# Layer 0's scaling of x reads the second copy of x, and the first copy's load waits for the dot products alone

## The reference, cut to what matters

```python
x = x_input                                   # (32, 512, 128)
e = (x @ a_i)[:, :, None] + (x @ a_j)[:, None, :]
mean = e.mean(axis=(1, 2)); var = ((e - mean) ** 2).mean(axis=(1, 2))
e = (e - mean) * rsqrt(var + 1e-14) * adj + adj
e = where(e >= 0, e, 0.2 * e)
alpha = softmax(e, axis=1)
h = sigmoid(einsum('bij,bjd->bid', alpha, x))
x = layernorm(x + h)
# layer 1: masked attention, a second aggregation and a small MLP, + x, layernorm
# layer 2: two projections mixed by a matrix made of adj, + x, layernorm
# layer 3: masked attention, elu, + x, layernorm
```

## Time and profile before

| what | value |
|---|---|
| median of the runs | 1194.18 us (1192.84 to 1195.81, 3 runs) |
| span of the profiled execution | 1188.6 us, 28920 instructions |
| TensorE matmul busy | 1103.5 us (93%) |
| VectorE busy | 1055.8 us (89%) |
| ScalarE busy | 964.7 us (81%) |
| GpSimd busy | 594.6 us (50%) |
| mean granted TensorE clock | 0.972 of full speed |
| loads of xA and xrA | 32 each, 256 KB, median 2.9 and 2.7 us to landing |

### The profile page before, as it was taken

How to read it: one execution, slowest core, us unless ns; L and a number is a source line. 1 busy time by engine, 2 the same in 40 slices (tenths; PEclk the granted TensorE clock), 3 DMA queues, 4 the chain that set the end, 5 groups by cost and what they waited for, 6 DMA issues and landing times.

```text
span 1188.6 us, 28920 instructions
## 1 busy us (share of the span) xinstructions
PE 1103.5 (93%) x7752; PEld 907.9 (76%) x7752; DVE 1055.8 (89%) x3894; ACT 964.7 (81%) x2453; POOL 594.6 (50%) x1250
## 2 busy tenths in 40 slices
PE   4779999999999999999999999999999999999964
PEld 3457777888777888887778888877778888788743
DVE  6887999999999999999999999999999899997642
ACT  3566888888888888888888889888888898888753
POOL 4243435555564555556555555555545554553422
PEclk7799999999999999999999999999999999999976
DMA  3010001110011111000111110101111010010000
GB/s 76 19 36 19 27 28 46 31 31 22 22 35 35 35 35 35 26 28 17 35 35 35 35 35 26 35 9 35 35 35 35 29 37 30 17 46 10 28 9 19
DMA packets 59478, 36.17 MB, mean 30 GB/s; under 512 B 3872, under 2 KB 54816, under 8 KB 59424
## 3 DMA queue, kind: packets, MB, share of 16 engines
q1 hardware_dynamic: 59424, 35.54, 10.0%
HBM read 18.75 MB, written 8.39 MB: 23 GB/s over the span
## 4 chain that ended last, share of the span: by engine, by line
PE 58%; POOL 10%; issue 9%; DVE 5%; ACT 2%; DMA 1%; POOLq 0%; SPq 0%; ACTq 0%; DVEq 0%
PE ps L965 14%; PE ps L893 7%; PE ps L949 6%; PE ps L982 4%; PE ps L1025 4%; PE ps L934 4%; PE ps L744 4%; PE ps L737 3%; POOL rirA L559 2%; PE ps L1014 2%; PE ps L880 2%; PE ps L1043 2%; PE ps L1042 2%; PE ps L919 1%; DMA xA<-in_x_dram 1%
## 5 line engine op out<-in xcount | busy, mean ns | idle before, releaser
L965 PE MATMUL ps<-hE,pTE 128*128 128x128 f32 x1024 | 131.0, 277 | 0.2
L982 PE MATMUL ps<-gin_j,hgat 128*128 128x512 f32 x256 | 124.4, 610 | 3.0 <-DVE gin_j L1495 1.8
L965 PE MATMUL ps<-hB,pTB 128*128 128x128 f32 x1024 | 125.3, 275 | 0.7 <-DVE pTB L1626 0.6
L893 PE MATMUL ps<-xsA,pA 128*128 128x128 f32 x1024 | 124.4, 275 | 0.0
L965 PEld LDWEIGHTS ps<-hE,pTE 128*128 128x128 f32 x1024 | 122.8, 193 | 0.9 <-issue 0.6
L1025 PE MATMUL ps<-att_j,xD 128*128 128x512 f32 x256 | 122.3, 601 | 0.8 <-ACT xD L2207 0.8
L965 PEld LDWEIGHTS ps<-hB,pTB 128*128 128x128 f32 x1024 | 119.4, 192 | 1.4 <-DVE pTB L1626 1.1
L893 PEld LDWEIGHTS ps<-xsA,pA 128*128 128x128 f32 x1024 | 119.4, 192 | 0.4 <-issue 0.3
L2250 ACT ACTIVATE pA<-vA,nmA,rirA 128x512 f32<-128x512 f32 x128 | 107.0, 845 | 6.3 <-DVE vA L1683 5.3
L2312 ACT ACTIVATE pE<-wE,mnE 128x512 f32<-128x512 f32 x128 | 92.4, 723 | 20.9 <-DVE mnE L1613 20.8
L1595 DVE SCALAR_TENSOR_TENSOR wE<-ps,hE,y2E 128x512 f32<-128x512 f32 x128 | 92.1, 739 | 13.8 <-ACT y2E L2282 13.7
(11 more groups left out here) (238 smaller groups left out, 3084.6 us busy)
## 6 DMA issues: line engine op xcount, KB each, us to landing
xA<-in_x_dram SPq DMA_DIRECT2D x32, 256.0 KB, 2.9
xrA<-in_x_dram SPq DMA_DIRECT2D x32, 256.0 KB, 2.7
xrB<-xB SPq DMA_DIRECT2D x32, 256.0 KB, 2.3
out_dram<-xout SPq DMA_DIRECT2D x32, 256.0 KB, 2.3
adj_i<-in_adj_dram SPq DMA_DIRECT2D x1, 1024.0 KB, 5.5
a<-in_L_gnn_a_dram SPq DMA_DIRECT2D x2, 64.0 KB, 5.1
w_sb<-in_L_gnn_W_dram SPq DMA_DIRECT2D x2, 64.0 KB, 3.7
l2w<-in_L_gnn_W_dram SPq DMA_DIRECT2D x2, 64.0 KB, 3.2
```

The lines of the kernel that those rows point to most:

```text
L893: last = mm(at("aggA")[:, i * P:(i + 1) * P], pA[:, j, i * P:(i + 1) * P], xsA[:, j], start=(j == 0), stop=(j == NT - 1))
L965: last = mm(at("agg" + n)[:, i * P:(i + 1) * P], att[n]["pT"][:, i, j], att[n]["h"][:, j, 0:P], start=(j == 0), stop=(j == NT - 1))
L982: last = mm(at("gin"), hgat[:, j], gin_j[:, j], start=(j == 0), stop=(j == NT - 1))
```

## The change

`load_xA` loses its wait for the scaling of the graph before. `scale_xA` reads xrA instead of xA, and waits for the load of xrA of its own graph. All orders of all engines stay as they are. Both copies hold the same data.

```diff
             def load_xA(g):
                 sp.wait_ge(s["stA_ready"], g.last)
-                sp.wait_ge(s["xA_scaled"], g.last)
                 sp.dma_start(xA[:], x_v[g.g]).then_inc(s["xA_in"], 16)
...
             def scale_xA(g):
                 act.wait_ge(s["rzA"], g.now)
+                act.wait_ge(s["xrA_in"], 16 * g.now)
                 act.wait_ge(s["aggA_ready"], g.last)
                 for j in range(NT):
-                    last = a.activation(xsA[:, j], xA[:, j], ACT.Copy, scale=rzA[:, j:j + 1])
+                    last = a.activation(xsA[:, j], xrA[:, j], ACT.Copy, scale=rzA[:, j:j + 1])
                 last.then_inc(s["xA_scaled"], 1)
```

## The result

The changed kernel takes 1197.66 us (median of 12 runs, 1193.45 to 1199.36), the kernel before 1193.18 us in the runs beside it (12 runs, 1189.72 to 1195.81). The ratio is 1.0039 with a 95% interval of 1.0026 to 1.0051, or 4.7 us slower (4.5 us by the two medians). In a second set of runs it was 1.0044 (1.0028 to 1.0059). The change makes the kernel slower by somewhat more than the 0.3% that can be told from none.

The account below looks back on a forecast made before the run. Prediction: TensorE, busy 93% of the span, bounds the kernel, so only its waits matter. Terms -0.3 - 0.9 + 1.9 + 3.2 - 0.2 give +3.7 us, +5.4 with one clock fall: 1199.6 us, range 1195.0 to 1203.1.

Parts of the forecast that it names:

- The rest around the span: Whole run: the median 1194.18 us exceeds the profiled span of 1188.6 us by 5.6 us, left unchanged in the forecast.
- The two stalls: Scalings of graphs 5 and 29 wait for late xrA, idle about 3 and 4 us: net +1.9 and +3.2 us.
- The terms for this piece: Behind the loop: graph 29's stall +3.2 us, a share of the +1.7 us clock fall, earlier xA for graphs 28 and 29 -0.2.
- Before the loop: Entry to the loop: graph 5's earlier xA -0.9 us, its scaling's stall +1.9 us, a share of the +1.7 us clock fall.
- Graph 5's earlier load: Before the loop: xA no longer waits for graph 4's scaling; gain between 0.57 and 1.25 us, taken as -0.9 us.
- The clock: TensorE's two new pauses: a fall to half clock costs 1.7 us; 0 to 3.4 us for both, one fall taken.
- The loop: Steady loop: xA's load leaves about 0.4 us sooner, but TensorE hardly waits for it; 0 to -1.2 us, taken as -0.3.
- a wait before L1656: Sign in the loop: VectorE would wait before the sum of squares instead, as its xA wait falls from 13.2 to under 5 us.

Follow-up runs that it names:

- e4: Changed kernel plus 14 extra matmuls on TensorE before its wait for graph 29's scaling, two waits exchanged: 1197.64 us, ratio 1.0017 to the kernel before.
- e3: Changed kernel with load_xrA(5) issued before keep_xB(4) and load_xrA(29) before keep_xB(28): 1187.84 us, ratio 0.9937 to the kernel before.
- e6: e3, but load_xA(5) again waits for graph 4's scaling and stands behind load_xrA(4): 1190.55 us, ratio 0.9972 to the kernel before.
- e10: The changed kernel run once more, unchanged, for a second profile: 1198.05 us, ratio 1.0044 to the kernel before.
- e2: Changed kernel with only the swap behind the loop, load_xrA(29) before keep_xB(28): 1194.49 us, ratio 0.9994 to the kernel before.
- e1: Changed kernel with only the swap before the loop, load_xrA(5) before keep_xB(4): 1194.52 us, ratio 0.9994 to the kernel before.
- e12: e8 plus 7 extra matmuls before TensorE's first sum behind the loop; two waits in sum_A exchanged, in the loop too: 1192.16 us, ratio 0.9994 to the kernel before.
- e8: e3 with xA loaded one place earlier in the loop, and earlier for graphs 29 and 30 behind it: 1187.95 us, ratio 0.9943 to the kernel before.
- e9: The kernel before run once more, unchanged, for a second profile: 1193.36 us, ratio 1.0003 to the kernel before.

## Why the prediction was right, and where its terms were off

The prediction was +5.4 us against the kernel before; measured are +4.7 and +5.3 us by the ratios (1.0039 and 1.0044 of 1194.18), 4.5 and 3.7 us by the medians of the two sets. In absolute time 1199.6 stands against 1197.66 and 1198.05, because the kernel before has since run at 1193.2 to 1194.8, and the three first runs were no better known than that.

*The rest around the span.* I took 5.6 us as lying outside the span. Wrong: the profiled execution of the changed kernel has a span of 1197.2 us and a time of 1198.93, so 1.7 us lie around it. The profile of before was of a quick execution, of about 1190.3 us. Since the rest was added unchanged, this did no harm.

*The two stalls.* Both came where and how the prediction said, with ScalarE's idle times of 3.21 and 4.72 us for "about 3 and 4". The landing behind the loop took 4.5 us in one trace and 4.8 in the other, where the earlier trace rows gave 4.0. From graph 28 to 31 the changed kernel took 107.3 us (two traces), the kernel before 102.7: 4.6 us more. The terms for this piece were 3.2 + half of 1.7 - 0.2, so 3.9. Without the clock they were right: e4, which keeps the stall and loses the fall, takes 105.68 us, 3.0 more than the kernel before, as forecast. The term sized too small was the clock's: both traces had a fall here, of 1.6 us, and half a fall was charged.

*Before the loop.* The terms were -0.9 (graph 5), +1.9 (stall) and half of 1.7: +1.9. The four traces that have this stall take 71.18 us from graph 4 to 6, the two of the kernel before 70.00: +1.2. Graph 5's earlier load is worth about 1.8 us and not 0.9: its piece, from graph 4's scaling to graph 5's, is 33.20 us in e3 and 34.67 and 35.28 us in the two traces of the kernel before. The step that failed is the bound: I had held that no more than VectorE's 1.25 us could come back, and e6 shows that TensorE's two waits, which add up to 1.55 in the earlier trace rows, do nearly all come back. The stall was sized well: 3.1 us against a kernel without it, less 1.4 us that came off before the sum of graph 6, is 1.7 where 1.9 was forecast. In three of the four traces a fall of 1.6 us came on top.

*The clock.* I took one fall for the two pauses. Of the seven long pauses in the traces that nothing fills (four before the loop, in after, e10, e2 and e4; three behind it, in after, e10 and e1) six were followed by a fall: both in the first profile of after, one in e10. The price of one is 1.6 us at both places, as taken (1.7). What was too small was their number: with three in four at the entry and three in three behind the loop the term is 2.9 us and not 1.7.

*The loop.* -0.3 us was forecast; -0.7 with a scatter as large is what the traces give. The turn stayed at 33.6 to 33.7 us, as said, but the reasoning was partly wrong. VectorE's wait for xA was to fall under 5 us and a wait before L1656 to take its place; it fell to 8.2, and no such wait came. The load leaves only 0.12 us sooner, not the 0.4 that I took. The 0.36 us of VectorE's mean wait that this should cover was for 0.315 its own jump. And a late xA costs through GpSimd's slots, 0.4 us in one turn of ten, not through TensorE's short waits for the dot products (e12).

*The sum.* Put beside the forecast in its own order, the traces give -0.7 (loop, for -0.3), -1.8 (graph 5, for -0.9), +1.7 (its stall, for +1.9), +3.0 (behind the loop, for 3.2 - 0.2) and +2.9 (clock, for +1.7): +5.1 us, where the forecast had +5.4. The two places, the order of events and the two stalls' sizes were worked out. That the whole came so near is in part luck: 1.3 us too little gain in the loop and at graph 5 stood against 1.2 us too little for the clock.

## What to carry to other kernels

When a step is moved to another copy of its data, look up for every iteration outside the steady loop when that copy is issued, and what stands ahead of it in its queue: here the loop itself gave some 0.7 us, and two iterations at its ends cost 9.5. If the new source then arrives late, move its load first and measure both together: with two lines swapped in SyncE's order the same change is 5 to 7.5 us faster than the kernel before, and moving xA's loads up as well (e8, 1187.95 us) is not measurably better. Before a wait is counted as something to win, find how much of the idle time is the engine's own.

## What the runs showed of the hardware

TensorE's clock does not follow from the length of a pause alone. The same wait behind the loop, 1.73 us, left the clock at 1.00 in after, and was followed by 0.50 in e3:

```profile
947.84 0.39 PE L859 MATMUL ps<-stA,nmean 128*128 128x8 f32 x2 [1.73 <-DVE prA L1640]
```
```profile
940.96 0.39 PE L859 MATMUL ps<-stA,nmean 128*128 128x8 f32 x2 [1.73 <-DVE prA L1640]
```
```profile
942.00:943.00 1.00, 1.00 (x3) 0.48 (x2) 0.96 (x6) 0.00 (x0) 0.73 (x2) 0.50 0.00 0
```

At the entry to the loop the pause of 2.62 us in e2 was followed by a fall, the one of 2.69 us in e10 was not. The three traces with over 4 us of pause behind the loop all had a fall there. Of the pause that every kernel has at 940 to 948 us the table's column "27 to 28" keeps a record: 36.0 to 36.3 us where the clock held, 36.9 to 37.5 us in the five executions where it fell. So a fall costs 0.9 to 1.4 us there, and 1.6 us at the two stalls. An even shorter pause, of 1.33 us at 118 to 121 us, stands in all 14 traces before the transposes (L737). In seven of them the clock fell within 3 us of it, in seven it did not; the former take some 1.3 us more from graph 2's scaling to graph 4's (65.4 to 65.9 us against 64.2 to 64.4). None of the seven is of the kernel before, which has two traces here; whether that is chance was not shown. Which execution meets a fall is a part of why executions of one kernel differ by 5 us and more. It is not the whole of it: the landings of xA are another part (e9).

An edit meant for one place behind the loop shifted GpSimd against VectorE by 0.05 us in every turn, and that moved this kernel by 6 us (e12). An experiment on a kernel that is tuned this tightly should leave the loop's instructions as they are, and its 20 turns should be read before its median is.
